# Self-attention in float32: two negated maxima on VectorE and the low part on GpSimd

## What is computed

```python
def mha(q, k, v):
    B, Nq, C = q.shape
    d = C // H                      # H = 16 heads, d = 32
    qh = q.reshape(B, Nq, H, d)
    kh = k.reshape(B, k.shape[1], H, d)
    vh = v.reshape(B, v.shape[1], H, d)
    scores = jnp.einsum('bqhd,bkhd->bhqk', qh, kh) / jnp.sqrt(jnp.asarray(d, q.dtype))
    attn = jax.nn.softmax(scores, axis=-1)
    out = jnp.einsum('bhqk,bkhd->bqhd', attn, vh)
    return out.reshape(B, Nq, C)
...
qkv = h @ qkv_w + qkv_b
q, k, v = jnp.split(qkv, 3, axis=-1)
h = mha(q, k, v) @ self_o_w + self_o_b
```

## Time and profile before

| | us |
|---|---|
| three runs, median | 4140.98 |
| lowest and highest of them | 4130.14, 4141.34 |
| the profiled execution, its own time | 4145.81 |
| its span (first to last instruction) | 4144.0 |
| TensorE busy with matmuls | 3766.3 (91%) |
| VectorE busy | 2335.7 (56%) |
| GpSimd busy | 2080.8 (50%) |
| ScalarE busy | 1877.2 (45%) |

### The profile page before, as it was taken

How to read it: one execution, slowest core, us unless ns; L and a number is a source line. 1 busy time by engine, 2 the same in 40 slices (tenths; PEclk the granted TensorE clock), 3 DMA queues, 4 the chain that set the end, 5 groups by cost and what they waited for, 6 DMA issues and landing times. The chain is left out here.

```text
span 4144.0 us, 51860 instructions
## 1 busy us (share of the span) xinstructions
PE 3766.3 (91%) x19596; PEld 2441.2 (59%) x19596; DVE 2335.7 (56%) x4020; ACT 1877.2 (45%) x3431; POOL 2080.8 (50%) x923
## 2 busy tenths in 40 slices
PE   4699969979999999999999999976999949999998
PEld 2577748844444444444444444425777737888887
DVE  1466642247777777777777777714666525222222
ACT  1465631115666666666666666653555521111111
POOL 0366630005778777787777777765576634000000
PEclk8798879978999999999999999997999869999999
DMA  7566657752130212102131201114666651211110
GB/s 224 139 160 173 169 159 221 226 135 62 26 67 16 64 26 56 37 16 64 26 67 26 59 22 26 31 47 111 145 177 156 163 168 54 73 40 40 40 40 30
DMA packets 213512, 371.45 MB, mean 90 GB/s; under 512 B 36104, under 2 KB 53000, under 8 KB 209704
## 3 DMA queue, kind: packets, MB, share of 16 engines
q1 hardware_dynamic: 213287, 368.49, 33.1%
HBM read 215.54 MB, written 144.51 MB: 87 GB/s over the span
## 5 line engine op out<-in xcount | busy, mean ns | idle before, releaser
L1952 DVE TENSOR_REDUCE a_peak<-a_sm 128x1 f32<-128x512 f32 x2048 | 1276.0, 683 | 448.9 <-PE a_sm L1792 445.4
L1906 ACT ACTIVATE a_e<-a_st 128x512 f32<-128x512 f32 x2048 | 1084.6, 597 | 686.3 <-PE a_st L1814 684.8
L2024 POOL TENSOR_TENSOR a_esum<-a_esum,a_e 128x2048 f32<-128x2048 f32 x256 | 1172.9, 4582 | 127.8 <-ACT a_e L1906 109.2
L1814 PE MATMUL a_st<-a_q,a_k 128*128 128x512 f32 x2048 | 868.3, 427 | 6.7 <-ACT a_e L1906 4.5
L1792 PE MATMUL a_sm<-a_k,a_q 96*128 96x512 f32 x2048 | 831.0, 413 | 47.5 <-DMA a_k<-s_k 28.0
L1814 PEld LDWEIGHTS a_st<-a_q,a_k 128*128 128x128 f32 x2048 | 386.0, 189 | 523.8 <-ACT a_e L1906 256.6
L1827 PE MATMUL a_acc<-a_e,a_v 128*32 128x512 f32 x4096 | 545.5, 605 | 15.1 <-ACT a_sums L1920 14.2
L1792 PEld LDWEIGHTS a_sm<-a_k,a_q 96*128 96x128 f32 x2048 | 396.9, 194 | 145.9 <-DVE a_peak L1952 55.5
L2147 PE MATMUL mlp_ph<-mlp_us,mlp_w_hi 128*128 128x512 f32 x1024 | 336.0, 390 | 32.6 <-DVE mlp_raw_lo L2196 32.6
L2189 ACT ACTIVATE mlp_gelu<-mlp_ph,mlp_b 128x512 f32<-128x512 f32 x128 | 88.3, 690 | 595.7 <-PE mlp_ph L2147 595.6
L2024 POOL TENSOR_TENSOR a_esum<-a_e 128x2048 f32<-128x2048 f32 x32 | 146.8, 4587 | 404.9 <-ACT a_e L1906 404.9
(11 more groups left out here) (151 smaller groups left out, 5171.7 us busy)
## 6 DMA issues: line engine op xcount, KB each, us to landing
p_qs<-s_q SPq DMA_DIRECT2D x192, 256.0 KB, 5.8
s_q<-p_qo SPq DMA_DIRECT2D x64, 512.0 KB, 7.6
a_q<-s_q SPq DMA_DIRECT2D x96, 256.0 KB, 5.0
a_k<-s_k SPq DMA_DIRECT2D x24, 1024.0 KB, 15.5
s_x<-p_x SPq DMA_DIRECT2D x16, 1024.0 KB, 4.3
s_u<-p_ut_hi SPq DMA_DIRECT2D x64, 256.0 KB, 6.0
s_u<-p_ut_lo SPq DMA_DIRECT2D x64, 256.0 KB, 6.5
p_us<-s_u SPq DMA_DIRECT2D x16, 1024.0 KB, 7.8
```

The source lines that it names most:

```text
L1814: pe.matmul(st[0:KR, place(kt, h) % RING], k[:, g % 2, h, kt * P:kt * P + KR], q[:, j % QR, h], start=True, stop=True).then_inc(score_done, 1)
L1906: act.activation(e[0:KR, (j * NKT + kt) % ER, h], st[0:KR, place(kt, h) % RING], ACT.Exp, scale=SCALE).then_inc(score_read, 1)
L1952: dve.tensor_reduce(dst, src, AX.X, ALU.max).then_inc(unit_read, 1)
L2024: pool.tensor_tensor(esum[:], e[:, slot(0)] if x == 1 else esum[:], e[:, slot(x)], ALU.add).then_inc(e_added, 1)
```

## The change

`minus_peaks` now writes the negated maximum twice, each time straight from the 64 columns of `peak` with a reduction that negates: once into the high columns of `neg`, whose type is now fp32r (rounded), and once in full into a new tile `minus`. The difference `minus` - high is taken by GpSimd in a new function `lower_parts`, into the low columns of `neg`. In GpSimd's step j it stands between add 7 and add 8, for the peaks of step j+1; for step 0 it stands ahead of all adds. The tiles `top` and `neg_hi` are gone. TensorE's transposes wait for GpSimd's result in place of VectorE's; VectorE's unit 0 waits until `minus` is written.

```diff
--- before.py
+++ after.py
@@ -1642,9 +1642,8 @@
         if POOLED:
             esum = sb("esum", [P, GH, W])
         peak = sb("peak", [P, U])
-        top = sb("top", [P, GH * TT])
-        neg_hi = sb("neg_hi", [P, GH * TT], F32R)
-        neg = sb("neg", [P, TT, P])
+        minus = sb("minus", [P, GH, TT])
+        neg = sb("neg", [P, TT, P], F32R)
         rows = sb("rows", [P, 2, W])
         sums = sb("sums", [P, 2, 2, W])
         den_t = sb("den_t", [P, W])
@@ -1657,7 +1656,7 @@
         rows_ready = [sem(f"rows_ready{r}") for r in range(QR)]
         k_loaded, v_loaded = [sem("k_loaded0"), sem("k_loaded1")], [sem("v_loaded0"), sem("v_loaded1")]
         unit_done, unit_read = sem("unit_done"), sem("unit_read")
-        top_done, neg_done, neg_ready = sem("top_done"), sem("neg_done"), sem("neg_ready")
+        neg_hi_ready, minus_ready, neg_lo_ready = sem("neg_hi_ready"), sem("minus_ready"), sem("neg_lo_ready")
         score_done, score_read, tile_used, e_added = sem("score_done"), sem("score_read"), sem("tile_used"), sem("e_added")
         divided, acc_read, scaled, spread = sem("divided"), sem("acc_read"), sem("scaled"), sem("spread")
         DIVIDES = 3 if NKT > 1 else 4
@@ -1695,6 +1694,10 @@
 
             units = [(j + 1, u) for u in range(HEAD, U)] + [(j + 2, u) for u in range(HEAD)]
             return [(m, u) for m, u in units if exists(i, m)]
+
+        def neg_part(x):
+
+            return neg[:, :, 3 * DH:3 * DH + 2 * GH].rearrange("p t (h s) -> p h t s", s=2)[:, :, :, x]
 
         def run(engine, step, first, late):
 
@@ -1795,11 +1798,11 @@
 
             def turn_peaks(i, j):
 
-                pe.wait_ge(neg_ready, 2 * (BODY * i + j + 1))
+                pe.wait_ge(neg_lo_ready, BODY * i + j + 1)
                 if j:
                     bank_free(pe, i, j - 1, TURN)
                 for qt in range(TT):
-                    mm = pe.transpose(st[:, TURN % RING if j else 0, qt * P:(qt + 1) * P], neg[:, qt], ident[:])
+                    mm = pe.transpose(st[:, TURN % RING if j else 0, qt * P:(qt + 1) * P], neg[:, qt].bitcast(F32), ident[:])
                 mm.then_inc(score_done, 1)
 
             def score_tile(i, j, kt, h):
@@ -1945,28 +1948,21 @@
             def peak_of_unit(i, j, u):
                 h, tiles, _ = UNITS[u]
                 if u == 0 and exists(i, j - 1):
-                    dve.wait_ge(neg_ready, 2 * (BODY * i + j))
+                    dve.wait_ge(minus_ready, BODY * i + j)
                 dve.wait_ge(unit_done, (BODY * i + j) * U + u + 1)
                 src = sm[:, bank_of_unit(j, u), 0:len(tiles) * KE].rearrange("p (x k) -> p x k", k=KE)[:, :, 0:KW]
-                dst = peak[:, u:u + 1] if KC > 1 else top[:, h * TT:(h + 1) * TT]
+                dst = peak[:, u:u + 1]
                 dve.tensor_reduce(dst, src, AX.X, ALU.max).then_inc(unit_read, 1)
 
             def minus_peaks(i, j):
 
                 n = BODY * i + j
                 dve.wait_ge(unit_read, (n + 1) * U + 2)
-                if KC > 1:
-                    dve.tensor_reduce(top[:], peak[:].rearrange("p (x c) -> p x c", c=KC), AX.X, ALU.max).then_inc(top_done, 1)
-                    dve.wait_ge(top_done, n + 1)
-                dve.tensor_scalar(neg_hi[:], top[:], -1.0, None, ALU.mult).then_inc(neg_done, 1)
-                dve.wait_ge(neg_done, n + 1)
                 if exists(i, j - 1):
                     dve.wait_ge(score_done, turned(i, j - 1) + 1)
-                by_head = lambda ap: ap.rearrange("p (h t) -> p h t", t=TT)
-                parts = neg[:, :, 3 * DH:3 * DH + 2 * GH].rearrange("p t (h s) -> p h t s", s=2)
-                dve.tensor_copy(parts[:, :, :, 0], by_head(neg_hi[:].bitcast(F32))).then_inc(neg_ready, 1)
-                dve.scalar_tensor_tensor(out=parts[:, :, :, 1], in0=by_head(top[:]), scalar=-1.0, in1=by_head(neg_hi[:].bitcast(F32)),
-                                         op0=ALU.mult, op1=ALU.subtract).then_inc(neg_ready, 1)
+                peaks = peak[:].rearrange("p (h t c) -> p h t c", h=GH, c=KC)
+                dve.tensor_reduce(neg_part(0), peaks, AX.X, ALU.max, negate=True).then_inc(neg_hi_ready, 1)
+                dve.tensor_reduce(minus[:], peaks, AX.X, ALU.max, negate=True).then_inc(minus_ready, 1)
 
             def divide(i, j, part):
 
@@ -2001,7 +1997,7 @@
 
             dve.sem_inc(unit_read, 2)
             dve.memset(ones[:], 1.0).then_inc(set_up, 1)
-            dve.memset(neg[:], 0.0).then_inc(set_up, 1)
+            dve.memset(neg[:].bitcast(F32), 0.0).then_inc(set_up, 1)
             if KE > KW:
                 dve.memset(k[0:3 * DH, :, :, keys:].bitcast(F32), 0.0).then_inc(set_up, 1)
             dve.wait_ge(set_up, SETUP)
@@ -2023,6 +2019,13 @@
                     pool.wait_ge(tile_used, n * NKT + ER)
                 pool.tensor_tensor(esum[:], e[:, slot(0)] if x == 1 else esum[:], e[:, slot(x)], ALU.add).then_inc(e_added, 1)
 
+            def lower_parts(i, j):
+
+                n = BODY * i + j
+                pool.wait_ge(neg_hi_ready, n + 1)
+                pool.wait_ge(minus_ready, n + 1)
+                pool.tensor_tensor(neg_part(1).bitcast(F32), minus[:], neg_part(0).bitcast(F32), ALU.subtract).then_inc(neg_lo_ready, 1)
+
             def scale(i, j):
                 n = BODY * i + j
                 pool.wait_ge(o_stored[j % 2], DMA * (BODY // 2 * i + j // 2 + 1))
@@ -2036,12 +2039,19 @@
                 if exists(i, j - LATE):
                     scale(i, j - LATE)
                 if POOLED and exists(i, j):
-                    for x in range(6, len(POOLED)):
+                    for x in range(6, 8):
+                        add(i, j, x)
+                if exists(i, j + 1):
+                    lower_parts(i, j + 1)
+                if POOLED and exists(i, j):
+                    for x in range(8, len(POOLED)):
                         add(i, j, x)
 
             pool.sem_inc(scaled, 2)
             pool.wait_ge(small_in, 2 * DMA)
             pool.tensor_copy(k[3 * DH:P, 1], mask[3 * DH:P].unsqueeze(2).to_broadcast([DH, GH, KC * KE])).then_inc(pool_set_up, 1)
+            pool.wait_ge(pool_set_up, 1)
+            lower_parts(0, 0)
             run(pool, step, LATE, LATE)
```

## The result

Six runs of the changed kernel gave a median of 4105.95 us (4100.01 to 4114.29), six of the kernel before 4138.36 us (4130.14 to 4141.34). The ratio is 0.9927, with a 95% interval of 0.9916 to 0.9939: 30 us less, between 25 and 35. The forecast was 26.5 us less, 4114.5 us, with a range of 4102 to 4126.

The account below looks back on a forecast made before the run. TensorE was taken as the bound, stalled 30 times by VectorE's unit reductions: 29 stalls at 0.90 us (26.1) plus 0.43 us give 26.5 us, taking the median from 4140.98 to 4114.5 us, range 4102 to 4126.

Parts of the forecast that it names:

- Reading L1961 as held: VectorE's negation of 16 elements, 1782 ns on average, is held until GpSimd's running addition is over.
- The two readings: TensorE's stall at VectorE's unit reductions: 0.64 us of shown idle time, or 0.90 us start to start, the one taken.
- The rival in which only the shown 19.4 us come back: At TensorE's 30 waits for VectorE's unit reductions, only visible idle time returns: 4121.6 us, chance 0.10.
- the stall of step 1: In step 1 L1961's hold is 1.37 in place of 1.84 us, so that stall is 0.43 us.
- The sum of 26.5 us: TensorE's self-attention stalls removed: 29 at 0.90 us, 26.1 us, and 0.43 us for step 1.
- The two reductions and their cover: VectorE's two reductions of 0.22 us are hidden before unit 0's matmul ends, with 0.9 us to spare.
- The other estimate: GpSimd's subtraction by the skill's rule of twice VectorE's time: some 0.37 us, where VectorE took 0.18.
- The rule that spoke against: By the rule alone, VectorE's second reduction is dearer: 220 against 180 ns, 31 times, 1.2 us lost.
- GpSimd's part as free of charge: The subtraction behind add 7 ends 2.4 us before the transposes, 1.9 at the bound; the path is charged nothing.
- The slower rival: GpSimd's result too late for the transposes; beyond 2.66 us of room each microsecond costs 31 us; 4173 us, chance 0.03.

Follow-up runs that it names:

- the second trace of before: The kernel before, unedited, profiled again: 4141.3 us (one run), self-attention stage 1772.5 us.
- the second set of runs: The changed kernel once more, unedited, against the kernel before: median 4109.14 us, ratio 0.9932 (0.9917 to 0.9947).

## Why the prediction was right

**The bound and the cause.** Reading L1961 as held, from two of its ends that met the ends of additions and one case with GpSimd idle, was the step that carried all. In the trace of before it ends 0.03 to 0.04 us behind the end of an addition in all 31 steps after step 0, and cutting add 7 shows the cause: 175 ns in every step. One reading of the page was a little off: by digits counted from 1, slice 10 (932 to 1036 us, with the first step and a half of the stage) shows 8 tenths, and not 9; its granted clock was 0.89, and 0.90 in the changed kernel, so nothing hangs on it.

**The size of the stall.** The two readings were 0.64 us of shown idle time and 0.90 us start to start. The stage gave 0.91. The rival in which only the shown 19.4 us come back is refuted by 27.3 us in both traces of the changed kernel, and by 26.0 us against the second trace of before. Over all steps the spacing of `weigh` from tile 11 to 12 had a median of 4.85 us before and 3.92 after, so 0.93 a stall; the stall of step 1 was 4.36 - 3.91 = 0.45 us, where 0.43 was foreseen. The sum of 26.5 us was short by 0.8, because the step that was read has 4.82 and lies a little below that median. This is less than the 1.3 us by which the two traces of before differ (in the second the median is 4.81), so that the sum came this close is in part luck. The two reductions and their cover came out as written, with 1.14 us of idle time where 0.9 was foreseen.

**GpSimd.** The subtraction was estimated at 0.23 and took 0.235 us. The other estimate, some 0.37 us for twice VectorE's time, was too high: VectorE, when not held, took 0.19 for the same subtraction. It ends 2.5 us ahead of the transposes (foreseen 2.4), and adds 8 and 9 did not slip: add 8 starts 0.29 us behind the end of add 7, as it did before.

**The rule that spoke against.** "VectorE: DVE Perf Modes" of the Trainium skill, Rules for kernel authors, advises against `tensor_reduce` on a hot path. The prediction priced that at 1.2 us for the second reduction; it took 0.21 us each time, in time in which VectorE would have stood idle, and cost nothing. "Advanced Engine Details and Errata" of the Trainium skill, VectorE Performance Modes, has the port shared and two-port instructions blocked. The runs agree for two kinds that its table gives a two-port mode, `tensor_scalar` (the negation, 1.85 us) and copy (1.57 us), and for reductions, to which it gives none: they were never held. In which mode an instruction ran no trace shows. The subtraction of two inputs has no two-port mode in that table and was held all the same.

**What I had not seen.** The prediction treats GpSimd's part as free of charge and does not ask whether it is needed. It carries 17.7 of the 27.3 us. The trace of before could not show that: L1968, with two inputs in SBUF, always ran in the 0.28 us in which GpSimd stood between two additions, because L1961 had waited out the first of them. "GPSIMD Engine Reference" of the Trainium skill, Key points, does name two SBUF inputs as a cause of contention; the run with the difference on VectorE agrees, with 1.68 us.

**The slower rival.** Its mechanism exists and its room was read rightly: one place later in the queue and TensorE waits. Its price was too low. It put 31 us on each microsecond of lateness in a step; the falls of the clock add about a quarter (94.5 us for some 76).

**The total.** Measured are 30 us less by the ratio, with 25 to 35 as the interval; the second set of runs gives 28 (22 to 34), and the stage 27.3. The rest is inside the scatter of the other stages. The median of 4105.95 us lies 8.5 us below the forecast of 4114.5; 2.6 us of that are the starting point alone, since the median of the kernel before over six runs is 4138.36 and not 4140.98.

## What to carry to other kernels

Suspect that a tiny instruction with a huge mean duration is being held, and find whose end its end meets. On VectorE, next to long GpSimd additions, put on the path only kinds that a trace shows unheld, and give what is left with two SBUF inputs to GpSimd itself, in a place of its queue where its result is early enough. Reductions are not the only such kind. In the kernel before VectorE also takes a reciprocal from SBUF to SBUF in the middle of GpSimd's first addition:

```profile
1130.87 0.24 DVE L1981 RECIPROCAL a_inv<-a_den_t 128x16 f32<-128x16 f32 x1
```

```profile
1129.39 4.59 POOL L2024 TENSOR_TENSOR a_esum<-a_e 128x2048 f32<-128x2048 f32 x1 [10.82 <-ACT a_e L1906]
```

It starts 1.5 us into the addition, 2.9 us before the addition ends, in 30 steps, and has at most 0.24 us in each.

Replace all the held kinds at once, or the hold moves to the next of them; and size a stall from start to start, in as many steps as there are.

## What was unexpected of the hardware

An idle gap of TensorE of about 2.2 us in an otherwise full stream was followed in 12 of 31 cases by a stretch at 1.2 GHz granted clock, at about 1.5 us each. A copy of 16 elements a partition on VectorE was held for 1.57 us by a GpSimd addition, a subtraction with two inputs for 1.68 us, whereas reductions of 64 elements were not held once. And `tensor_reduce` writes a rounded type into strided columns at the 0.22 us of the plain one.
